# Attention and edge convolutions in one kernel: SP's transfers of the second half's division put ahead of the load of x and the write of the tiles

## The reference

```python
q = h @ wq.T; k = h @ wk.T; v = h @ wv.T                 # 1x1, all channels
dw = lax.conv_general_dilated(qkv, dw_kernel, ...)       # 5x5, each channel alone
pw = lax.conv_general_dilated(dw, pw_kernel, ...)        # 1x1 in groups of 8
qkv_all = jnp.concatenate([qkv, pw], axis=1)             # plain heads, then convolved ones
scores = jnp.einsum('bhdn,bhen->bhde', value_pad, key_)  # value_pad: one row of ones more
out = jnp.einsum('bhde,bhen->bhdn', scores, query)
out = out[:, :, :-1] / (out[:, :, -1:] + EPS)            # the division
y = lax.conv_general_dilated(out, proj_kernel, ...)      # then batch norm, and + x
```

## Time and profile before

| | us |
|---|---|
| median of 3 runs | 5295.28 (5291.56 to 5298.55) |
| the profiled execution | 5290.55 |
| its span, first to last instruction | 5288.7 |
| PE busy (share of the span) | 4903.9 (93%) |
| DVE busy | 2567.7 (49%) |
| ACT busy | 2019.4 (38%) |
| mean granted clock of PE | 0.975 of 2.4 GHz |

### The profile page before, as it was taken

How to read it: one execution, slowest core, us unless ns; L and a number is a source line. 1 busy time by engine, 2 the same in 40 slices (tenths; PEclk the granted TensorE clock), 3 DMA queues, 4 the chain that set the end, 5 groups by cost and what they waited for, 6 DMA issues and landing times. The chain is left out here.

```text
span 5288.7 us, 65292 instructions
## 1 busy us (share of the span) xinstructions
PE 4903.9 (93%) x22760; PEld 3450.8 (65%) x22760; DVE 2567.7 (49%) x3635; ACT 2019.4 (38%) x3671; POOL 1197.2 (23%) x1030
## 2 busy tenths in 40 slices
PE   8999999999999999999999996899999989998958
PEld 7887887887887887887887884344344434443423
DVE  3333333333333333343243331587588578847865
ACT  3332332332332332333333330355555455545555
POOL 2331341341431431431331330000200020011002
PEclk9999999999999999999999998999999999999969
DMA  6665565565665575565565564344344243424313
GB/s 185 195 208 193 191 208 191 193 214 188 195 214 179 189 228 178 190 226 180 189 227 182 182 211 164 128 137 133 124 134 150 103 148 128 160 100 142 114 43 113
DMA packets 390815, 893.16 MB, mean 169 GB/s; under 512 B 33488, under 2 KB 66512, under 8 KB 388240
## 3 DMA queue, kind: packets, MB, share of 16 engines
q1 hardware_dynamic: 390544, 889.18, 51.0%
HBM read 588.74 MB, written 300.32 MB: 168 GB/s over the span
## 5 line engine op out<-in xcount | busy, mean ns | idle before, releaser
L734 POOL TENSOR_TENSOR toeplitz<-taps 128x512 f32<-128x512 f32 x768 | 863.0, 1152 | 1005.0 <-PE bank L442 1005.0
L442 PEld LDWEIGHTS bank<-toeplitz,columns 128*128 128x128 f32 x8192 | 956.1, 192 | 14.1
L442 PE MATMUL bank<-toeplitz,columns 128*128 128x128 f32 x8192 | 957.1, 275 | 0.0
L1030 PE MATMUL bank<-att,w_proj 128*128 128x512 f32 x2048 | 909.5, 598 | 34.2 <-DVE centred L1315 23.8
L1030 PEld LDWEIGHTS bank<-att,w_proj 128*128 128x128 f32 x2048 | 392.9, 192 | 531.8 <-issue 523.3
L357 PE MATMUL bank<-x_hi,w_hi 128*128 128x512 f32 x1536 | 614.4, 400 | 76.0 <-DVE x_lo L601 76.0
L359 PE MATMUL bank<-x_lo,w_hi 128*128 128x512 f32 x1536 | 603.5, 393 | 0.0
L358 PE MATMUL bank<-x_hi,w_lo 128*128 128x512 f32 x1536 | 602.8, 392 | 0.0
L1363 POOL TENSOR_TENSOR centred<-centred,x_out 128x512 f32<-128x512 f32 x128 | 164.6, 1318 | 1933.8 <-ACT centred L1177 1933.8
L1043 PE MATMUL bank<-edge,w_branch 128*128 128x512 f32 x1024 | 493.1, 627 | 96.7 <-ACT edge L1131 96.7
L672 DVE TENSOR_SCALAR ckey_t<-bank 128x256 f32<-128x256 f32 x256 | 108.4, 423 | 905.2 <-PE bank L442 905.1
(11 more groups left out here) (115 smaller groups left out, 5635.3 us busy)
## 6 DMA issues: line engine op xcount, KB each, us to landing
x_sb<-in_x_tiled SPq DMA_DIRECT2D x128, 1024.0 KB, 6.1
tiles_dram<-tiles SPq DMA_DIRECT2D x128, 867.0 KB, 4.2
loaded<-tiles_dram SPq DMA_DIRECT2D x256, 433.5 KB, 4.1
inverse<-inverse_dram SPq DMA_DIRECT2D x256, 256.0 KB, 4.7
att_dram<-out_sb SPq DMA_DIRECT2D x256, 256.0 KB, 4.4
att<-att_dram SPq DMA_DIRECT2D x64, 1024.0 KB, 6.3
xb<-x_dram SPq DMA_DIRECT2D x128, 330.0 KB, 3.2
x_out<-in_x_pad SPq DMA_DIRECT2D x32, 1056.0 KB, 5.2
```

What stands on the lines that cost most here:

```text
L442: last = nc.tensor.matmul(bank[:, v * M:(v + 1) * M], columns[:, h % 2, t - T_K, v + b, a * HT:(a + TO) * HT], w[:, t, d, :], start=(d == ...
L734: last = nc.gpsimd.tensor_tensor(toeplitz[:, h % 2, t, :].rearrange("p (d o r) -> p d o r", o=HD, r=PL), tap, point, ALU.mult)
L1030: last = nc.tensor.matmul(P_BANKS[m][:, :], w_proj[:, i * HALF + k, m * P:(m + 1) * P], att[:, i, k, :], start=(i == 0 and k == 0), stop=( ...
```

## The change

In `plain`, SP's round j is written in another order. Before, it was: load of x, write of the tiles, then everything that belongs to the division. Now the write of the inverse (j = 2), its first two loads (j = 3) and the spills with the loads behind them (j = 4 to 7) come first, then the load of x and the write of the tiles; `write_w` and `load_w_proj` stay behind. Spills 6 and 7, which stood behind the loads of the first heads, are now in round 7, ahead of the last write of the tiles.

```diff
                 def plain(it, conv_of):
                     for j in range(NCH):
-                        if j + XR < NCH:
-                            sp.wait_ge(qkv_ready, 3 * (NCH * it + j + 1))
-                            load_x(it, j + XR)
-                        write_tiles(it, j)
                         if conv_of is not None:
                             if j == 2:
                                 write_inverse(conv_of, 1)
...
+                            if j >= 4:
+                                for i in range(2 * j - 8, 2 * j - 6):
+                                    spill(conv_of, 1, i)
+                                    if i + 2 < NCH:
+                                        load_inverse(conv_of, 1, i + 2)
+                        if j + XR < NCH:
+                            sp.wait_ge(qkv_ready, 3 * (NCH * it + j + 1))
+                            load_x(it, j + XR)
+                        write_tiles(it, j)
+                        if conv_of is not None:
                             if j == 4:
                                 write_w(conv_of, 1)
                             if j == 6:
                                 load_w_proj(it, 0)
-                            if 4 <= j < NCH - 1:
-                                for i in range(2 * j - 8, 2 * j - 6):
-                                    spill(conv_of, 1, i)
-                                    load_inverse(conv_of, 1, i + 2)
...
                     for h in range(LR):
                         load_head(h)
-                    if conv_of is not None:
-                        for j in range(NCH - 2, NCH):
-                            spill(conv_of, 1, j)
```

## The result

The changed kernel takes 5197.5 us (median of 4 runs, 5192.1 to 5202.3) where the kernel before took 5293.4 beside it: ratio 0.9819, 95% interval 0.9802 to 0.9836.

A forecast was written before the change was run, and what follows sets the result against it. PE, busy 93% of the span, was taken as the bound, held up in chunks 4 to 6 by DVE's late inverse. Terms -78.4 + 6 - 1.5 = -73.9 us gave 5221 us, range 5207 to 5245 for the likeliest case.

The forecast's parts named there:

- (f): End of `plain`: 1.5 us gained on waits for keys; PE's issue waits at `conv` taken as 0, bounds 0 and -6.6.
- (a): Inverse's write, round 2: issued some 3 us earlier, its wait over 2.9 us before the load of x, costing nothing.
- (b): Inverse loads 0 and 1, round 3: issued near 842 instead of 851.25, so DVE's 5.35 us wait goes.
- (c): Spills and loads, rounds 4 to 6: waits on `divided` cost nothing, margin 2.7 us; inverse waits like 5.84 us go.
- (d): PE then waits for x in chunks 4 to 6: spare 1.5 us, tightest 0.4; floor of 29.90 us reached.
- (e): More traffic ahead of x in chunks 4 to 6: x delayed 0.8 us, stalling 0.4 an iteration, 6 us in all.
- the forecast's own sign for (e): x landing later than S' + 5.5 (S' the next chunk's start on PE), with ACT and PE waiting, would show mis-sizing.
- the third case: Rival "No change": x late by 2.9 us, stalls of 5.3 us an iteration, 5295 us; chance 0.04.
- the slower case: Rival: SP's new waits hold the load of x; at 3.5 us late, stalls total 106 us, giving 5321 us; chance 0.03.
- (g): `conv`, the last iteration and `edges` keep their order: 0 us.
- traffic takes half back: Rival, chunks 4 to 6: x lands 2.0 us later, stalls of 39 us in all, 5254 us; chance 0.09.
- SP stands in front of the load of x: Rival: new waits on `divided` hold SP's load of x; slower from 2.9 us on, 5321 us at 3.5; chance 0.03.

The follow-up runs named there:

- e3: The kernel before, with only the inverse's write (round 2) and its loads 0 and 1 (round 3) moved ahead of the load of x: 5296.5 us, ratio 1.0007.
- e4: The kernel before, with only the spills of rounds 4 to 6 and the loads behind them moved ahead of the load of x: 5299.8 us, ratio 1.0007.
- the second profile: The changed kernel run once more, unaltered, beside the kernel with spills 6 and 7 put back: 5194.2 us, ratio 0.9815.
- e7: The changed kernel with two more 256 KB transfers ahead of the load of x in rounds 4 to 6: 5223.2 us, ratio 0.9866.
- e1: The changed kernel with spills 6 and 7 put back behind the loads of the heads: 5206.6 us, and 5205.4 when run again.
- e2: The kernel before, with only spills 6 and 7 moved ahead of the last write of the tiles: 5282.4 us, ratio 0.9976.
- e6: The changed kernel with four extra 256 KB memory-to-memory transfers behind the loads of the first heads: 5206.6 us, ratio 0.9825.
- e5: The changed kernel with the spills and inverse loads of rounds 4 to 7 between the load of x and the tiles' write: 5259.6 us, ratio 0.9928.
- e8: The changed kernel with only the spills moved behind the load of x, the inverse loads staying ahead of it: 5265.2 us, ratio 0.9939.

## Why the prediction was wrong

The direction and the mechanism of chunks 4 to 6 were right; the size was 22 us too small, and nearly all of that comes from term (f), the end of `plain`. Step by step:

(a), (b), (c): right. In the fifth iteration the inverse's write goes at 815.95 and the load of x behind it at 818.81; loads 0 and 1 go at 820.03, the load of x behind them at 829.63. SP's spills and loads of round 4 stand at S + 4.1 to 5.7, the load of x at S + 8.6; DVE divides at S + 2.7 with no wait. What I had not seen is that (b) and (c) are no terms of a sum: e3 and e4, which do one of them each, gain nothing.

(d): right. PE reaches the floor of 29.90 in most iterations, with x split 2.60 us beside POOL and some 0.3 us to spare in chunk 5.

(e): the sum was right in the first profile by luck, the mechanism was not. The forecast was 6 us of stall left, and 455.0 - 448.5 = 6.5, but 0.9 in the second profile. I had x late by 0.8 us and PE by 0.4 in every iteration. In 14 of the 15 iterations ACT had the x for chunk 6, which is issued behind the four transfers, 6.2 to 6.9 us after its issue; before the change it was 6.1 in the earlier trace rows. So it came late by 0.9 us or less, and PE did not wait for it. The stall sits in a few iterations, 4.1 of the 6.5 us in one. In the second iteration x was issued at 256.67 and ACT had it at 265.68, 9.0 us later; PE then stood for 2.11, the window's clock was 0.95 and it took 34.00 us. That is the forecast's own sign for (e): x landed at S' + 7.7, not by S' + 5.5. Why in this iteration and not in the others stays open. SP's load, ACT, PE:

```profile
256.67 0.41 SPq L190 DMA_DIRECT2D x_sb<-in_x_tiled  x1
```
```profile
265.68 2.01 ACT L485 ACTIVATE x_hi<-x_sb 128x512 fp32r<-128x512 f32 x2 [3.52 <-DMA x_sb<-in_x_tiled]
```
```profile
270.35 0.50 PE L356 MATMUL bank<-x_hi,w_hi 128*128 128x512 f32 x1 [2.11 <-DVE x_lo L600]
```

The rule weighed there (the Trainium skill, DMA: Bandwidth & Descriptors, Queues, rings and completion order) fits e4, where x took 8.6 us with 1 MB issued in the 2.4 us ahead of it, and e7; it costs next to nothing in the changed kernel, where x took 6.2 to 6.9 us. There the same 1 MB is issued 3 to 4.5 us ahead, and that most of it has gone by then is my reading.

Three readings in the weighing of (e) were wrong. All four transfers still ahead of x would be a delay of 4.2 us; the third case, to which the text sends it, has 2.9, and by its way of reckoning 4.2 is slower than the slower case's 3.5. The argument that x already lands in 6.1 us behind the division's traffic does not hold: the x of the earlier trace rows was issued at 849.02, ahead of loads 0 and 1 (851.25) and of all spills. And the bytes of the stretch did not stay the same.

(f): **the step that failed**, a term of the sum put at nothing. I put PE's issue waits at the head of `conv` at 0, "since nothing shows that the two are linked", and bounded them at -6.6 by taking the smallest, 0.97 us, for a floor. They are linked to the two spills (e1, e2) and a part seems to come back with other traffic in their place (e6), and the floor is zero: all 20.2 us went. The stretch gave 19.6 where the forecast had 1.5. Why the waits are 20.2 us in the kernel before and 2.0 in e4, both with the spills there, is not shown. Two things should have warned me. The same stretch in the first iteration has the same loads of heads and no spills, and no issue wait: it takes 23.3 us (87.1 to 110.4) against 25.2 on average in the 15 others, 28.5 us over in all; I used that iteration as the floor for chunks 4 to 6 and not here (there PE enters the loop and doesn't jump back to it, which would have been a reason to doubt, not to ignore it). And the bound needed a reason for its floor, not just the smallest value seen.

(g): right within 1 us; 1.8 us more of the gain is chance in the first iteration. Of the 97.8 us from the forecast's 5295.3 to 5197.5 another 4 remain over, within the spread of the runs.

The rivals: "traffic takes half back" and "SP stands in front of the load of x" did not come about in the changed kernel, but both exist, e7 and e4. That the range's lower end came from the bound in (f) is why one wrong term put the time outside it.

## What to carry to other kernels

An order of transfers on one queue is worth judging as a whole: here two halves of the change gave nothing each and about 88 us together, since a stall that is removed at one chunk comes back at the next as long as that chunk's transfers stand behind the large ones, and one long stall was followed by a low clock more often than two short ones (e3). Put a transfer ahead of a wait that is certain to end later (here spills at S + 4 ahead of a load that can't go before S + 8.7), and check by the timeline that its own wait ends first. And keep the queue clear where the loop jumps back to other code: add up every stretch between two marks, against an iteration without the work, before putting a wait there at nothing or calling its smallest value a floor.

## What the runs showed of the hardware

- PE's "issue" wait at the head of the loop's body is not a constant. With two spills of 256 KB behind the loads of the heads it is 20.2 us in 14 pieces (before), 9.4 in 9 and 12.7 in 11 (e1), 8.4 in 8 (e3) and 2.0 in 4 (e4); with 1 MB of other traffic there 4.5 in 4 (e6); without either 3.7 in 3 (e2) and none in five profiles (changed twice, e5, e7, e8).
- Two divisions of DVE take 1.99 us alone (changed) and 4.70 us beside POOL's building of the weights (e5), and the split of x 1.76 and 2.60 (both changed). When a wait moves DVE's work onto POOL's, the delay grows.
- Behind a stall of PE the clock falls to 1.2 GHz for a part of the stretch in some iterations: in 5 of 15 with two stalls of 1.0 to 2.4 us (before), in all 14 that have one of 2.3 to 2.9 us in e5, and in all 15 with one of 3.3 to 3.8 (e3). The length does not settle it: in e8 the clock fell behind a stall of 2.79 us in one iteration and stayed at full behind one of 2.79 in another. Near the end of `plain` it falls behind three waits of 1.5, 0.8 and 1.0 us in none to 9 of 15 iterations. There a fall costs 1.7 us, read from 25.40 against 23.70 above. So a stall's price here is its length and often some 1.7 us more.
- The DMA engines moved 247 GB/s in chunks 4 to 6 before, 307 in the changed kernel and up to 356 in e7, and x issued behind 1 MB took 8.6 us when that was issued in the 2.4 us ahead (e4), mostly 6.2 to 6.9 when it was issued 3 to 4.5 us ahead (changed).
